# Relational graph attention on one core: 80 chunks instead of 70 fed by the walk, eight walk blocks beside each of the first 45, slot numbers loaded one at a time between matmuls

## What is computed

```python
h_proj = jnp.einsum('nd,rde->rne', h, relation_weight)
t_r = h_proj[etype, src]
h_r = h_proj[etype, dst]
att = jnp.sum(t_r * jnp.tanh(h_r + efeat), axis=-1)
...
a = att_exp / denom[dst]                      # softmax over the edges of one dst
h_nb = jax.ops.segment_sum(h[src] * a[:, None], dst, num_segments=N)
out = leaky_relu((h + h_nb) @ res_w1.T) + leaky_relu(h * h_nb @ res_w2.T)
```

## Time and profile before

| | |
|---|---|
| median of three runs | 10518.47 us (10516.94 to 10518.93) |
| profiled execution | 10518.84 us, span 10517.0 us |
| mean granted clock of TensorE | 0.516 |
| busy: PE / PEld / DVE / ACT / POOL | 3213 / 2869 / 4730 / 2636 / 7749 us |
| stage 2, far chunks | from 490 to about 4090 us |
| stage 2, near chunks | to about 6270 us |

### The profile page before, as it was taken

How to read it: one execution, slowest core, us unless ns; L and a number is a source line. 1 busy time by engine, 2 the same in 40 slices (tenths; PEclk the granted TensorE clock), 3 DMA queues, 4 the chain that set the end, 5 groups by cost and what they waited for, 6 DMA issues and landing times. The chain is left out here.

```text
span 10517.0 us, 77420 instructions
## 1 busy us (share of the span) xinstructions
PE 3213.4 (31%) x16334; PEld 2868.5 (27%) x16500; DVE 4729.7 (45%) x5151; ACT 2635.5 (25%) x2314; POOL 7749.0 (74%) x8165
## 2 busy tenths in 40 slices
PE   5567777777777774000000013000000000000001
PEld 2256766667676764000000003000000000000001
DVE  4455555555555556778777775111111111111113
ACT  3212222222222222222222224222222222222221
POOL 3677777777777777777777765777777777777776
PEclk8755555555555555555555555555555555555555
DMA  9967777777777776444444441111111111111111
GB/s 364 322 164 181 180 182 179 178 180 181 178 183 181 180 180 162 137 128 132 134 128 137 128 115 42 52 51 54 51 54 51 51 54 51 54 51 54 51 51 52
DMA packets 1330242, 1325.37 MB, mean 126 GB/s; under 512 B 1053304, under 2 KB 1099288, under 8 KB 1317130
## 3 DMA queue, kind: packets, MB, share of 16 engines
q1 hardware_dynamic: 1038169, 748.56, 27.8%
q0 software_dynamic: 254688, 368.09, 15.0%
q10 hardware_dynamic: 37344, 208.28, 5.1%
HBM read 781.03 MB, written 543.26 MB: 126 GB/s over the span
## 5 line engine op out<-in xcount | busy, mean ns | idle before, releaser
L1204 POOL DMA_INDIRECT gs<-table,idx_s x3125 | 3008.2, 963 | 994.1 <-issue 974.2
L1568 POOL DMA_INDIRECT gy<-ytab,idx x3125 | 2951.6, 945 | 1011.3 <-issue 951.8
L1512 PEld LDWEIGHTS banks<-win,pick 128*125 128x125 f32 x9900 | 2150.7, 332 | 338.2 <-issue 312.7
L1512 PE MATMUL banks<-win,pick 128*125 (+1 forms) x9900 | 2121.1, 413 | 186.8 <-DVE pick L1260 185.7
L1603 DVE TENSOR_TENSOR_SCAN run<-keep,add 128x1664 f32<-128x1664 f32 (+1 forms) x126 | 453.2, 3597 | 3016.4 <-ACT add L1633 3016.4
L1208 POOL DMA_INDIRECT gd<-table,idx_d x1375 | 1363.7, 992 | 419.0 <-issue 419.0
L540 PE MATMUL ps_cm<-tail,mask_m 128*128 128x64 f32 x196 | 43.6, 423 | 4007.2 <-DVE mask_m L475 4007.2
L540 PEld LDWEIGHTS ps_cm<-tail,mask_m 128*128 128x128 f32 x196 | 42.3, 331 | 4008.5 <-DVE mask_m L475 4008.5
L1633 ACT COPY add<-gy 128x1600 f32<-128x1600 f32 (+1 forms) x126 | 400.8, 3181 | 2353.8 <-DMA gy<-ytab,idx 2353.8
L1496 PE MATMUL banks<-hi,lo 128*128 128x98 bf16 x3125 | 278.8, 283 | 2004.4 <-DVE hi L1247 2004.4
L1496 PEld LDWEIGHTS banks<-hi,lo 128*128 128x128 bf16 x3125 | 263.9, 145 | 2019.3 <-DVE hi L1247 2019.3
(11 more groups left out here) (263 smaller groups left out, 4671.8 us busy)
## 6 DMA issues: line engine op xcount, KB each, us to landing
proj_d<-found SPq DMA_DIRECT2D x330, 512.0 KB
win<-table SPq DMA_DIRECT2D x660, 240.0 KB
table<-rows SPq DMA_DIRECT2D x98, 1536.0 KB, 8.8
sums<-rowbuf ACTq DMA_DIRECT2D x124, 825.0 KB
ef<-in_edge_attr_dram SPq DMA_DIRECT2D x125, 800.0 KB, 4.5
sums<-rowbuf ACTq DMA_DIRECT2D x124, 800.0 KB, 3.5
keyb<-step_keys SPq DMA_DIRECT2D x332, 234.4 KB, 5.5
gd<-proj_d SPq DMA_DIRECT2D x70, 800.0 KB, 5.9
```

The source lines that it names most:

```text
L1204: pool.indirect_dma_start(out=gs[:, s, g, :], out_offset=None, in_=table_vec, in_offset=bass.IndirectOffsetOnAxis(ap=idx_s[:, s, g:g + 1], ...
L1512: nc.tensor.matmul(acc[k][0:MT, bass.ds(slots[t] * D, D)], pick[:, w, t * MT:(t + 1) * MT], win[:, w, bass.ds(at_w, 1), :].rearrange("p o ...
L1568: pool.indirect_dma_start(out=gy[:, s, g, :], out_offset=None, in_=ytab, in_offset=bass.IndirectOffsetOnAxis(ap=idx[:, s, g:g + 1], axis=0 ...
```

## The change

`FAR` goes from 55 to 45 and `PER` from 6 to 8: 45 far chunks with 8 walk blocks each (360 blocks), 80 near chunks. The batched load of 16 slot numbers (L1501) is replaced by 16 single loads, function `slot_of`. Those for block b+1 are placed in the walk of block b, one behind each of its 15 products and one more after them; those for the first block of a chunk are placed behind 16 of the histogram's 25 matmuls; the last walk of a chunk holds none. `win` and `pick` have two buffers instead of three. DVE's picks move: four in `front`, then after the edge feature, after the scores, after `edge_rows`, after the one-hots. ACT's copies of walk results move accordingly. In stage 1 `node_high` shares memory with `kk`, and the pieces of the table work between searches are cut a little differently; with 360 blocks the list of steps takes 43 columns instead of 39 (`UC`).

```diff
-FAR = 55
+FAR = 45
-PER = 6
+PER = 8
-KSLOTS, WSLOTS = 4, 3
+KSLOTS, WSLOTS = 4, 2
...
-            node_high = sb(c1, "node_high", [P, TILE_OF, NB], BF16)
+            node_high = kk[:, :, :].rearrange(...)[:, TILE_OF * P // 2:TILE_OF * (P + NB) // 2].bitcast(BF16)...
...
                     def front(c, s, i, link, far=False):
-                        if far:
-                            picks(c, s, i, 0)
...
                         if far:
-                            picks(c, s, i, 1)
+                            for j in range(4):
+                                picks(c, s, i, j)
...
                         if far:
-                            picks(c, s, i, 2)
+                            picks(c, s, i, 4)
...
-                        if far:
-                            picks(c, s, i, 3)
...
                         if far:
-                            picks(c, s, i, 4)
+                            picks(c, s, i, 5)
...
                         if far:
-                            picks(c, s, i, 5)
+                            picks(c, s, i, 6)
                         if go_on:
                             low_hots(c + 1, link)
                             high_hots()
+                        if far:
+                            picks(c, s, i, 7)
...
+                    def slot_of(b, t):
+                        return nc.values_load(pe_tab[0:1, bass.ds(16 * b + t, 1)], engines=[mybir.EngineType.PE], min_val=0, max_val=K,
+                                              skip_runtime_bounds_check_because=MADE)
+
-                    def histogram(c):
+                    def histogram(c, ahead=False):
+                        slots = []
                         pe.wait_ge(onehot_ready, c + 1)
                         for g in range(G):
                             last = nc.tensor.matmul(hist, lo[:, g, :], hi[:, g, :], start=False, stop=False)
+                            if ahead and G - 18 <= g < G - 2:
+                                slots.append(slot_of(PER * c, g - (G - 18)))
...
-                    def walk(c, j):
+                    def walk(c, j, slots):
                         b, k, w = PER * c + j, j % 2, j % WSLOTS
-                        _, slots = nc.values_load_multi_w_load_instructions(
-                            pe_tab[0:1, bass.ds(16 * b, 16)], engines=[mybir.EngineType.PE], min_val=0, max_val=K,
-                            skip_runtime_bounds_check_because=MADE)
+                        ahead = []
...
                                              win[:, w, bass.ds(at_w, 1), :].rearrange("p o d -> p (o d)"), start=False, stop=False)
+                            if j < PER - 1:
+                                ahead.append(slot_of(b + 1, t))
+                        if j < PER - 1:
+                            ahead.append(slot_of(b + 1, K))
```

More of the change, by code:

```diff
@@ L689, in gnn_program @@
             node_low = kk[:, :, :].rearrange("p u e -> p (u e)")[:, 0:TILE_OF * P // 2].bitcast(BF16).rearrange("p (k j) -> p k j", j=P)
-            node_high = sb(c1, "node_high", [P, TILE_OF, NB], BF16)
+            node_high = kk[:, :, :].rearrange("p u e -> p (u e)")[:, TILE_OF * P // 2:TILE_OF * (P + NB) // 2].bitcast(BF16).rearrange("p (k j) -> p k j", j=NB)
             ps_n = ps(c1, "ps_n", [P, 3, NB])
@@ L1008, in _ @@
                     search(0)
-                    for q, (n0, n1) in enumerate(((17, 18), (18, 19), (19, 20), (20, 22), (22, 23)), 1):
+                    for q, (n0, n1) in enumerate(((17, 18), (18, 20), (20, 21), (21, 22), (22, 23)), 1):
                         part(dve, quarters, n0, n1)
@@ L1432, in chunk @@
                             take_found(PER * c, 0)
+                            take_found(PER * c + 1, 1)
                         if t0:
@@ L1442, in chunk @@
                         if far:
-                            take_found(PER * c + 1, 1)
+                            take_found(PER * c + 2, 0)
                         act.wait_ge(exp_arg, k + 1)
@@ L1452, in chunk @@
                         if far:
-                            take_found(PER * c + 2, 0)
+                            take_found(PER * c + 3, 1)
                         if follows:
@@ L1463, in chunk @@
                         if far:
-                            take_found(PER * c + 3, 1)
                             take_found(PER * c + 4, 0)
+                            take_found(PER * c + 5, 1)
+                            take_found(PER * c + 6, 0)
                     chunk(0, 0, 0, True)
@@ L1496, in histogram @@
                             last = nc.tensor.matmul(hist, lo[:, g, :], hi[:, g, :], start=False, stop=False)
+                            if ahead and G - 18 <= g < G - 2:
+                                slots.append(slot_of(PER * c, g - (G - 18)))
                         last.then_inc(onehot_used, 1)
-                    def walk(c, j):
+                        return slots
+                    def walk(c, j, slots):
                         b, k, w = PER * c + j, j % 2, j % WSLOTS
-                        _, slots = nc.values_load_multi_w_load_instructions(
-                            pe_tab[0:1, bass.ds(16 * b, 16)], engines=[mybir.EngineType.PE], min_val=0, max_val=K,
-                            skip_runtime_bounds_check_because=MADE)
+                        ahead = []
                         if j >= 2 or later(c):
@@ L1518, in walk @@
                                          start=False, stop=True).then_inc(found_mm, 1)
-                    histogram(0)
+                        return ahead
+                    slots = histogram(0, True)
                     for j in range(PER):
-                        walk(0, j)
+                        slots = walk(0, j, slots)
                     with pe.Fori(1, FAR) as c:
-                        histogram(c)
+                        slots = histogram(c, True)
                         for j in range(PER):
-                            walk(c, j)
+                            slots = walk(c, j, slots)
                     with pe.Fori(FAR, CHUNKS) as c:
```

## The result

The changed kernel takes 11767.24 us in the median of four runs (11763.89 to 11772.86) against 10518.34 us: a ratio of 1.119, 95% interval 1.117 to 1.121. It is 1249 us slower. 11,470 had been forecast, in a range from 10,700 to 12,050.

What follows compares the result with a forecast made beforehand. POOL paced the kernel before; afterwards PE's sequencer would, at 34.9 + 1.2 + 52.9 + 5.0 = 94.0 us a far chunk. 44 x 94.0 - 3184.5 = +952 us on 10518.8 gives 11,470 us, range 10,700 to 12,050.

Steps and rivals of the forecast that it cites:

- POOL paces both kinds of chunk, 335 us to be had: Stage 2: POOL's indirect DMAs pace far (64.7 us) and near (31.2 us) chunks; ten far turned near can give 335 us.
- The sequencer is the bound, the array has slack: PE in far chunks: a walk's 8.25 us is the in-order sequencer's work, slot loads block; the array needs only 7.6 us.
- Sequencer outside the loads, 36.1 us: PE's sequencer per new far chunk: eight walks without loads, 34.9 us, plus histogram and loop, 1.2 us.
- One load 0.41 us, and 5 us of contention: 57.9 us: PE's 128 single slot loads per far chunk, with address and gap: 52.9 us, plus 5 us from SP's work beside them.
- No address: Rival on PE's slot loads: the 16 addresses cost nothing beside one common base; P = 81.2, +388 us, 10,907 us; chance 0.14.
- Batch price: Rival: each single load costs a sixteenth of the batch, contention included; P = 76.6, +186 us, 10,705 us; chance 0.07.
- Hidden: Rival: a single load lets PE's sequencer go on, so the array bounds the walk; P = 66, -280 us, 10,238 us; chance 0.10.
- Long loads: Rival: each PE single load behaves like SP's 0.89 us load; P = 168, about 14,700 us; chance 0.07.
- Picks, copies and buffers cost nothing: Far chunks: moved DVE picks, ACT copies and two buffers are covered at 11.4 us a walk; no cost.
- Stage 1: nothing, with 5 us as upper end: Stage 1: four more gathers into `kk` cost at most 4.9 us; taken as 0.

Runs made afterwards that it cites:

- the run with words: Changed kernel with slot table in 32-bit words, block j in partition j, one batched load of 16 words per walk, no unpacking: 10184.35 us, ratio 0.968.
- the first experiment: Changed kernel, but each walk reads its 16 slot numbers with one batched load at its start, as before: 10745.66 us, ratio 1.022.
- the batch run: Changed kernel with the batched load of 16 byte slot numbers put back at each walk's start: 10745.66 us, ratio 1.022.
- the packed run: Changed kernel, but each walk reads its 16 one-byte slot numbers as four 32-bit words in one batched load and unpacks them in registers: 10303.13 us, ratio 0.980.
- the address left out: Changed kernel, but every single load reads a fixed place of the slot table, without address computation (sums wrong): 11196.67 us, one run.
- loads by fours: Changed kernel with byte slots still loaded ahead between matmuls, but four at a time, four loads a walk instead of sixteen: 10864.01 us, one run.

## Why the prediction was right, and where it was off

- *POOL paces both kinds of chunk, 335 us to be had.* Right; the run with words collects it.
- *The sequencer is the bound, the array has slack.* Right, and it gave the sign. Putting the loads between matmuls hid nothing, because the batch had been overlapped with the array already.
- *Sequencer outside the loads, 36.1 us.* In the changed kernel 100.4 less the loads' 64.4 leaves 36.0. With batches it is 5 us more; that did not enter the forecast but did enter the first experiment's.
- *One load 0.41 us, and 5 us of contention: 57.9 us.* This is the term that was mis-sized. Measured (records of the sequencer over 30 chunks): a load 0.343 in the mean, 0.064 to the next instruction, 0.096 for the address, together 0.503, or 64.4 us. Of the 6.5 us more, 1.8 are the load itself (0.287 against SP's 0.273), 3.1 the gap behind it (0.04 taken from SP), 2.1 slow loads (7.1 against 5.0), less 0.5 for the address. Times 44 that is 286 of the 297 us between forecast and result. Chunk 0 adds 25; the 0.1 us a chunk outside the loads, the near part and what follows it take off about 8, and the profiled executions are 5 us further apart than the medians.
- *Bounds and rivals.* No address: the address instructions are there and worth 13 us a chunk. Batch price: a single load costs 0.50 us all told, and not the 0.277 of a sixteenth of a batch. Hidden: the sequencer stands still for each load. Long loads: the median is 287 ns, so 0.89 us does not hold on PE here. Nor does the floor of about 600 ns that the Trainium skill gives in "DMA: Bandwidth & Descriptors", section "Latency and other measured facts".
- *Picks, copies and buffers cost nothing.* Right at 12.5 us a walk. At 9.6 us, in the batch run, and at 8.4 us, in the packed run, ACT's copy costs the sequencer about 3 us a chunk; picks and buffers still cost it nothing that the traces show.
- *Stage 1: nothing, with 5 us as upper end.* Wrong by its own bound: stage 2 starts 13.7 us later. Against 1249 us this is small.

## What to carry over

Before moving an instruction "into the shadow" of matmuls, look at the sequencer's rows, not the array's: if a loop's period equals the sum of its sequencer's instructions and the short gaps between them, with no waits, everything there costs its full length wherever it stands, addresses included. Count how far apart two undisturbed iterations start and subtract. That number predicted three of these runs within 1% (single loads in the kernel before, the address left out, loads by fours). It missed the batch by 1.9%, since it leaves out the waits that appear once the sequencer is ahead. And before moving a register load, look at the type of what it reads.

## What the runs showed of the hardware

- A register load depends on the element type: 16 byte elements 3.79 us, 16 words 1.12; 4 bytes 0.99, 4 words 0.33; one byte 0.287 on PE, one word 0.27 on SP. Each byte adds some 0.234 us; 16 words come to 0.07 each. The Trainium skill, "Runtime: NRT & Kernel Launch", section "Instruction fetch mechanics", has about 200 ns per register even in bulk, where it speaks of the registers that are loaded at launch; the slot table here is in SBUF. The bytes come near that figure, the words do not.
- The clock granted to TensorE stayed at 0.50 of full speed, 1.2 GHz, in the far part while PE was 0.73 busy (kernel before) and even 0.86 (after). In the run with words it was 0.58 in the mean with PE 0.87 busy, so part of that stretch was at 2.4 GHz. With words in the kernel before it was 0.58 too, with PE only 0.66 busy (490 to 4046 us). No run held this apart, and POOL's pace hid what it gave.
